# Three score buffers in the head loop of a ViT tower kernel, and two small ScalarE steps on GpSimd

## What is computed

```
qkv = h @ W_qkv[i];  q, k, v = split into 16 heads of 64
kr  = r @ W_r[i]
AC  = einsum(q + u, k);  BD = einsum(q + v, kr)
prob = softmax((AC + BD) / 8)
h = layer_norm(h + (prob @ v) @ W_o[i]) * g1 + b1
h = layer_norm(relu(h @ W_ff1[i] + b_ff1) @ W_ff2[i] + b_ff2) * g2 + b2
```

## Time and profile before

| | us |
|---|---|
| median of 3 runs | 2784.75 |
| lowest and highest of them | 2784.02, 2785.15 |
| the profiled execution | 2779.74 |
| span of that execution, first to last instruction | 2777.6 |

### The profile page before, as it was taken

One profiled execution on the slowest core, in us unless ns is written; L12 is line 12 of the kernel. 1 busy time (PEld: TensorE's weight loads), 2 busy tenths in 40 slices (PEclk: granted clock), 3 DMA queues, 4 the chain that ended last, 5 costly groups with the idle time before them and its releaser, 6 DMA issues. The chain is left out here.

```text
span 2777.6 us, 61222 instructions
## 1 busy us (share of the span) xinstructions
PE 2232.7 (80%) x19212; PEld 1644.3 (59%) x19213; DVE 1803.0 (65%) x5446; ACT 1618.7 (58%) x5077; POOL 1189.3 (43%) x2202
## 2 busy tenths in 40 slices
PE   0168988988789988988888889888889989833995
PEld 0146666666566666666566666665666666522663
DVE  8746777776567777766667777766677777633333
ACT  2146767766557767765666666666666666611221
POOL 3045555554355555544455555544554454202002
PEclk9589999999999999999999999999999999965998
DMA  5353333434543333354433333344333333155002
GB/s 166 91 143 90 97 92 95 98 95 140 161 112 93 93 92 93 92 153 108 135 99 95 95 94 92 94 144 146 97 95 97 95 98 95 40 146 175 28 28 76
DMA packets 387569, 289.49 MB, mean 104 GB/s; under 512 B 45256, under 2 KB 360768, under 8 KB 385856
## 3 DMA queue, kind: packets, MB, share of 16 engines
q1 hardware_dynamic: 380800, 268.87, 36.8%
q10 hardware_dynamic: 4864, 12.68, 1.3%
q0 software_dynamic: 1600, 4.23, 0.5%
HBM read 125.54 MB, written 59.09 MB: 66 GB/s over the span
## 5 line engine op out<-in xcount | busy, mean ns | idle before, releaser
L1197 ACT ACTIVATE E<-E,nb 128x257 f32<-128x257 f32 x1024 | 514.3, 511 | 83.6 <-DVE nb L1363 83.6
L1363 DVE CUSTOM_DVE_ANT_0 E<-bk,cb 128x257 f32<-128x257 f32 x1024 | 390.6, 418 | 107.9 <-PE bk L1012 107.5
L917 PE MATMUL bk<-hin,w_sb 128*128 128x257 f16 x3072 | 428.8, 277 | 17.1 <-ACT rel L1131 9.3
L1325 DVE TENSOR_TENSOR pt<-bk,pt 128x512 f16<-128x512 f32 x512 | 354.1, 692 | 70.1 <-ACT pt L1184 61.9
L965 PE MATMUL bk<-ident,E 128*128 128x128 f32 x2048 | 323.8, 281 | 87.6 <-ACT E L1197 61.0
L917 PEld LDWEIGHTS bk<-hin,w_sb 128*128 128x128 f16 x3072 | 298.5, 99 | 75.7 <-ACT rel L1131 14.5
L813 POOL TENSOR_SCALAR rq<-rel 128x257 f16<-128x257 f32 x256 | 104.6, 409 | 525.5 <-ACT rel L1131 525.2
L965 PEld LDWEIGHTS bk<-ident,E 128*128 128x128 f32 x2048 | 221.8, 141 | 169.4 <-ACT E L1197 152.5
L1184 ACT ACTIVATE pt<-bk 128x512 f16<-128x512 f32 x512 | 307.7, 601 | 10.3 <-PE bk L965 10.0
L1011 PE MATMUL bk<-kh,qs 128*128 128x257 f16 x1024 | 258.5, 278 | 47.7 <-DMA hin<-hd_dram 47.5
L1012 PE MATMUL bk<-kl,qs 128*128 128x257 f16 x1024 | 258.5, 278 | 0.0
(11 more groups left out here) (270 smaller groups left out, 4386.3 us busy)
## 6 DMA issues: line engine op xcount, KB each, us to landing
qs<-rq SPq DMA_DIRECT2D x256, 128.5 KB, 3.5
kh<-rk SPq DMA_DIRECT2D x256, 128.5 KB, 3.3
kl<-rk SPq DMA_DIRECT2D x256, 128.5 KB, 3.6
wf<-in_w_dram SPq DMA_DIRECT2D x168, 128.0 KB, 2.4
w_split_dram<-wh SPq DMA_DIRECT2D x168, 128.0 KB, 2.1
wf<-in_we_dram SPq DMA_DIRECT2D x96, 128.0 KB, 2.2
we_split_dram<-wh SPq DMA_DIRECT2D x96, 128.0 KB, 1.7
w_sb<-w_split_dram SPq DMA_DIRECT2D x12, 1024.0 KB, 7.0
```

Source lines behind the costliest of these rows:

```text
L917: r = mm(bank[4 + s % 2][:, 0:S], wcol(a, C_QKV, k, 3 * HD, chunk_at(s)), hin[:, m, k, :], start=i == 0, stop=i == 5)
L1197: act.activation(E[:, h % 2, qt, :], E[:, h % 2, qt, :], ACT.Exp, bias=nb[:, 2 * h + qt:2 * h + qt + 1], scale=-1.0, accum_out=sums[:, qt, ...
L1325: v.tensor_tensor(pt[:, h, 1, :, 0:IMG], bank[2 + h % 2][:, :].rearrange("p (k s) -> p k s", k=QT), pt[:, h, 0, :, 0:IMG], ALU.subtract).t ...
L1363: v.tensor_tensor_reduce(E[:, h % 2, qt, :], bank[qt][:, 0:S], cb[:, h, :], -SCORE, 3e38, ALU.add, ALU.min, nb[:, 2 * h + qt:2 * h + qt + ...
```

## The change

The score buffers become three. Head h uses `sq` if h % 3 = 2, and otherwise `E[:, h % 3]`. DVE therefore waits, from head 3 on, for the transposes and the class column of head h-3 and not of head h-2. The class column leaves ACT's queue for POOL's, behind the split of slot h, as a `tensor_copy`. LN2's high half leaves ACT's queue (h = 8) for POOL's (h = 7), as two `tensor_scalar` by 1, and after the last body likewise.

```diff
+        scores = lambda h: sq[:, :, :] if h % 3 == 2 else E[:, h % 3, :, :]
...
+            def ln2_hi(at):
+                pool.wait_ge(hd_out, at(16, -16))
+                for k in range(KC):
+                    pool.wait_ge(z2_ok, at(2, k - 1))
+                    pool.tensor_scalar(hout[:, 0, k, :], x[:, k, :], 1.0, 1.0, ALU.mult, ALU.mult).then_inc(z2_hi, 1)
+
+            def class_column(at, h):
+
+                pool.wait_ge(e_ok, at(32, 2 * h + 2))
+                pool.tensor_copy(ecol[:, :, class_row(h, 0):class_row(h, 3):4], scores(h)[:, :, CLS:S].broadcast_to([P, QT, 3])).then_inc(ecol_ok, 1)
...
                 for h in range(H):
                     for s in slots(h, kind):
                         split_projection(at1, s)
+                    class_column(at, h)
...
                     if h == 5 and kind.ln2:
                         ln2_gain(at)
+                    if h == 7 and kind.ln2:
+                        ln2_hi(at)
...
             ln2_gain(At(pool, L * B))
+            ln2_hi(At(pool, L * B))
...
-                                         E[:, h % 2, qt, kt * P:(kt + 1) * P], ident[:, :])
+                                         scores(h)[:, qt, kt * P:(kt + 1) * P], ident[:, :])
...
-            def ln2_hi(at):
-                act.wait_ge(hd_out, at(16, -16))
-                for k in range(KC):
-                    act.wait_ge(z2_ok, at(2, k - 1))
-                    act.activation(hout[:, 0, k, :], x[:, k, :], ACT.Copy).then_inc(z2_hi, 1)
...
-                        act.activation(E[:, h % 2, qt, :], E[:, h % 2, qt, :], ACT.Exp, bias=nb[:, 2 * h + qt:2 * h + qt + 1],
+                        act.activation(scores(h)[:, qt, :], scores(h)[:, qt, :], ACT.Exp, bias=nb[:, 2 * h + qt:2 * h + qt + 1],
...
-                    if h == 8 and kind.ln2:
-                        ln2_hi(at)
...
-                    act.wait_ge(e_ok, at(32, 2 * h + 2))
-                    act.activation(ecol[:, :, class_row(h, 0):class_row(h, 3):4], E[:, h % 2, :, CLS:S].broadcast_to([P, QT, 3]), ACT.Copy).then_inc(ecol_ok, 1)
...
-            ln2_hi(At(act, L * B))
...
-                    if h >= 2:
-                        v.wait_ge(t_done, at(16, h - 1))
-                        v.wait_ge(ecol_ok, at(16, h - 1))
+                    if h >= 3:
+                        v.wait_ge(t_done, at(16, h - 2))
+                        v.wait_ge(ecol_ok, at(16, h - 2))
...
-                        v.tensor_tensor_reduce(E[:, h % 2, qt, :], bank[qt][:, 0:S], cb[:, h, :], -SCORE, 3e38,
+                        v.tensor_tensor_reduce(scores(h)[:, qt, :], bank[qt][:, 0:S], cb[:, h, :], -SCORE, 3e38,
```

## The result

The changed kernel is slower: 2795.04 us median of 6 runs against 2783.55 of the kernel before, also 6, a ratio of 1.004 with a 95% interval of 1.0028 to 1.0053. That is +11.5 us. The forecast was slower by 29.0, with a range of 2790 to 2845. The time lies inside the range, the sign and the place were right, and the size was 2.5 times the measured one.

What follows compares the result with a forecast made beforehand. ACT was taken to bound the head loop, with POOL's gapless stretch ending last after the change. 26.2 + 5.7 - 1.5 - 2.2 + 0.8 = +29.0 us on the 2784.75 median gave 2813.7 us, range 2790 to 2845.

Steps and rivals of the forecast that it cites:

- The bound: Full image's head loop: ACT sets the pace, busy 28.46 of 28.84 us; POOL runs 17.4 us without a gap.
- The path to head 14: Slot 11's split end, then DVE's queue, to ACT's exponential of head 14: 1.90 us; exponential 1.19 later, loop 1.09 longer.
- The price of the class column: POOL's queue: each class column costs c = 0.20 us, range 0.1 to 0.3; nine stand in a full image's stretch.
- LN2's high half: POOL's stretch: two one-input instructions of 257 elements add 0.80 us; ACT drops 0.62.
- 240c - 19: Whole kernel: total change in us as a function of the class column's cost c on POOL; +29.0 at c = 0.20.
- the entry images: Three images where PE's `class_v` follows POOL's copy: 1.9 us later each, 5.7 in all.
- Closing images: Three images: first eight heads gain 0.8 us, last eight lose 0.8; together 0, give or take 1 each.
- The third buffer: DVE's wait for PE's transposes in the head loop: gain nothing, upper bound ACT's 0.35 us at head 8.
- A, ACT stays the bound: Rival: POOL takes the additions in its 7.2 us of idle time per loop; -65 us, 2720; chance 0.10, including part.
- B, a dearer copy: Rival: POOL's class column costs more than 0.20; +53 us at c = 0.3, +139 at 0.66; chance beyond 0.3: 0.09.
- C, near the break-even: Rival: c near the memset's 0.10 on POOL; +5 us, 2790; chance 0.05, with anything else within 5.6 us.
- the 0.01 that the chances name for c: Example for a part of the rival that ACT stays the bound: sum -17 us, 2768; chance 0.10 with that rival.

Runs made afterwards that it cites:

- a mere change of order: Against the run with class columns split between POOL and ACT and the high half on ACT: LN2's normalisation and gain spread over slots 4 to 6; 2753.73 us, 0.9889.
- the run with two copies: Changed kernel plus a second copy of the same 6 elements on POOL before each class column, into an unread spare tile; 1.017 of the kernel before.

## Why the prediction was wrong in size and right in kind

**The bound.** Right. ACT's busy share of the full loop (28.46 of 28.84 us) pointed to the right engine; but the second chain, POOL's stretch with DVE's queue behind it, was 1.21 us short of ACT's at head 14, and this decided the case. At head 8 it was the later one already. The idle time of ACT came at heads 8, 10, 12 (before `take_q`) and 14, 2.47 us in all, where some 3 us at heads 8, 10, 13 and 14 were forecast.

**The path to head 14.** Right. Its 1.90 us behind the split was 1.87. With the measured terms its own formula gives the measured loop: the stretch grew by 19.33 - 17.38 = 1.95 us and starts 0.20 earlier (0.18 by the rows), so head 14's exponential comes 922.65 + 1.95 - 0.20 + 1.90 - 925.76 = 0.54 later, and less the one column behind it the loop ends 0.44 later; the traces show 0.41.

**The price of the class column: the step that failed.** I took c = 0.20. The copy lasts 0.195 us (mean over 512), so the duration was right. But what counts is what it adds to the queue. It starts 0.06 us before the record of its predecessor ends, and the next instruction starts 0.15 after it (907.81 to 907.96). Before the change the same split stood so:

```profile
905.76 0.64 POOL L815 TENSOR_TENSOR rq<-rel,rq 128x257 f16<-128x257 f32 x1
906.37 0.41 POOL L813 TENSOR_SCALAR rk<-rel 128x257 f16<-128x257 f32 x1
```

From its second half to the next split it was 0.61; now it is 0.74 (907.22 to 907.96), so the copy adds 0.13 here, and over the nine in the stretch (1.95 - 0.74) / 9 = 0.134 each. The prediction did look at a distance from start to start, 0.19 at 920.23 to 920.42. That distance held a wait. The split behind it is that of slot 10, whose `take_q` had only just ended in the kernel before:

```profile
919.80 0.47 ACT L1131 ACTIVATE rel<-bk,u 128x257 f32<-128x257 f32 x1
```

It ends at 920.27, and the split starts 0.15 later. The splits of slots 12 and 14, which wait for their `take_q` by the trace's own word, start 0.16 and 0.15 after its end (923.27 plus 0.48 to 923.91, 926.75 plus 0.49 to 927.39). Where `take_q` is long done, the same copy is 0.15 to 0.16 from its successor: 923.54 to 923.69 in the changed kernel (line 863), and so in the run with the high half alone, where POOL has no class column at all:

```profile
920.24 0.20 POOL L863 COPY hcls<-hout 128x4 f16<-128x4 f16 x1
920.40 0.41 POOL L815 TENSOR_SCALAR rq<-rel 128x257 f16<-128x257 f32 x1
```

The trace of before had it too: in the loops of the three closing images `take_q` is done over 1 us ahead, and the distance is 0.16. So of the error of 0.066 us, 0.04 were this wait, and the rest is that POOL starts the copy 0.02 to 0.03 us sooner after the split than it would start the next instruction (in the medians over the full loops 0.06 us before the split's record ends, for 0.03). The right principle was at hand as well: the prediction itself counted ACT's column at 0.096 for its duration of 0.20, and didn't ask whether POOL overlaps its starts as well.

**LN2's high half.** 0.80 predicted, 0.74 measured (918.79 to 919.53), a second and smaller error of size.

**The leverage.** Nine columns in each of 24 loops: the sum is 240c - 19, and its slope turned 0.066 us of error into 16 us. With c = 0.134 and 0.74 for the high half, the term of a full image is 0.44 for 1.09, 10.5 for 26.2 in all, that of the entry images 3.9 for 5.7, and the sum becomes 11.5. Measured: 11.5. That it fits so well is in part luck, as the terms below show.

**The terms, measured.** The 24 full images +11.2 for 26.2 (0.4 in most of them, but +2.0 in one whose granted clock is 1.00 in the run before and 0.96 in the run after, so that about 1.6 us of the sum can't be laid to the change). Opening image 28.61 to 26.69, -1.9 for -1.5, at a granted clock of 0.95 and 0.97. Final image -2.1 for -2.2. Entry images +1.1, +2.0 and +1.3, 4.4 in all for 5.7, on loops in which the granted clock isn't the same in the two runs (0.94 and 0.96 in the first of them). Closing images +1.0, -0.5 and -0.3 for 0; these loops differ by as much between runs of other kernels here (37.02 and 38.12 in the second of them, before and with the third buffer alone), so nothing is read from them. From the last loop's end to the end of the last LN2 +0.8 for +0.8. What lies before the first loop (-1.0), between the loops (+0.2) and behind the last LN2 (-0.4) was taken as nothing.

**The third buffer.** Taken as worth nothing, and alone it is. That it would be worth 1.3 us per full loop once POOL makes the column, the prediction didn't say; it only showed that with three buffers the new wait costs nothing beyond the split's. The new wait does come up (0.68 us of DVE's idling before head 13), but ACT reached head 13 later by its own wait for POOL in `take_q`, and so that part holds.

**The rivals.** A, ACT stays the bound: out, with 2.47 us of idling. B, a dearer copy: out. C, near the break-even: nearest to what happened, as c = 0.134 lies between its 0.10 and the forecast's 0.20, though the 11.5 us are clear of its 5.6; the range's lower end of 2790 was set by that 0.10. No run shows the 0.01 that the chances name for c, with a sum of -17: the copy of six float32 elements lasts 0.195 us, about as long as the one of four float16 elements (0.202), and adds 0.134 to the queue.

## What to carry to other kernels

An engine with a low busy share can still be the bound over a part of a loop, as POOL was at head 8 of the kernel before, busy for 43% of the span and for 21.64 us of the loop's 28.84. Before work is moved onto it, find its longest stretch without a gap, follow what waits for the stretch's end through the in-order queues, and compare with the time at which the bounding engine gets there; the difference is the whole budget, for all moves together. Do so at each place where the two chains meet: here it was 1.21 us at head 14 and nothing at head 8, and a mere change of order that relieved head 8 gained 0.72 us per loop. Two moves that gain by themselves can lose together (here gains of 0.55 and 0.39 us and a loss of 0.40 per full loop), so they are measured apart and jointly. And the price of a small instruction, here 0.134 us for a record of 0.195, is what it adds to the distance between the starts of its neighbours, read where the next one waits for nobody.

## What the runs showed of the hardware that I had not expected

A GpSimd copy of 6 float32 elements per partition lasts 0.195 us (mean over 512 in the changed kernel), and starts about 0.06 us before its predecessor's record ends, so that it adds only 0.13 to 0.14 us to a full queue, and a second one right behind it 0.12. In the run with two copies the one whose output has a stride of 4 elements lasts 0.193 to 0.194 us, and the same copy into the packed spare tile 0.188 to 0.189, 0.005 less. GpSimd's split that waits for ScalarE's `take_q` mostly starts 0.15 to 0.17 us after that record's end (median 0.158 in the kernel before, 0.161 in the changed one). In the kernel before, ScalarE's small copy of the same data had a record of 0.20 to 0.26 us (median 0.215) and took 0.09 to 0.10 of the queue.
